# The last pass of a wide cross attention also prepares the feed-forward's first tokens and weights

## Chip, cores and metric

One core of a Trainium2 chip runs the whole program. The metric is the device time of one execution in microseconds. The engines are PE (TensorE), DVE (VectorE), ACT (ScalarE), POOL (GpSimd) and SP (SyncE, which issues the transfers). L12 is line 12 of the kernel.

## The reference

Six residual blocks run over x, 32 sequences of 64 tokens, 512 wide, each on layer-normalised tokens (`_layernorm`):

```python
x = x + _L0_attn_ref(_layernorm(x), ...)             # attention, weights by sign
x = x + _L0_xattn_ref(_layernorm(x), ctx_4096, ...)  # 32 heads of 128, 8 key heads, q and k by RMS norm
x = x + _L0_ffn_ref(_layernorm(x), c1_w, c2_w, w1, w2t)
x = x + _L1_attn_ref(...)
x = x + _L1_xattn_ref(...)
x = x + _L1_ffn_ref(...)
```

The block behind the change's boundary is the third:

```python
inter = xf @ c1_w.T @ c2_w.T                 # rank 16, 1792 wide
blk = inter.reshape(B * T, 56, 32)
idx = argmax(blk, -1) + arange(0, 1792, 32)  # one hidden unit of each 32
h = relu(einsum('bkm,bm->bk', w1[idx], xf))
out = einsum('bk,bkm->bm', h, w2t[idx])
```

## The kernel before

The 2048 tokens stay in one SBUF tensor X, 16 tiles of 128 tokens. A group is four tiles (512 tokens), `ST` = 4. Every product in full precision is made of rounded operands: a float32 matrix is kept as a rounded part ("hi", type fp32r, written by ACT) and what is left ("lo", by DVE or POOL), and three matmuls (hi·hi, hi·lo, lo·hi) make one product (`products`, L93).

The program is a row of blocks: `small_attention` ("sign"), `cross_attention`, `sparse_ffn`, `small_attention` ("alibi", "cross", and the experts). Each block writes one instruction list for each engine by hand, and the order in it is fixed. An engine waits on semaphores. Between blocks all engines wait for each other, so nothing of a block starts before the last instruction of the block before has ended on every engine.

`cross_attention` (L1945) runs 16 passes (`PASSES`): two halves of 1024 tokens (two groups each) by eight key heads. A pass loads Wq and Wo for its head through one landing buffer `raw`, each split by ACT (`wq_keep`, Wo at L2184) and POOL (`low`, L2205). Its two steps of 512 tokens make four query heads of products (`head`), their sums of squares, scores, softmax, values and then eight output products `output(0)` to `output(7)` of twelve matmuls (L2520). DVE adds each to X (`add_y`, L2327). So in pass 15 all of X's first group has been final since pass 7. A second landing buffer, `raw_kv`, takes key and value weights for two passes and the context halves; from pass 14 on it holds nothing that is still to come. `PT` takes the turned probabilities up to the end.

`sparse_ffn` (L1153) makes four passes, one for each group. A pass has 16 slots, four tiles by four quarters of 448 hidden units: PE makes the rank product (`rank_product`, L1493) one slot ahead, then H(s), the hidden product of slot s (12 matmuls on W1), then turns the kept h of slot s-2 (L1526), then the second-layer product of slot s-4 (`second`, L1471). DVE finds each block's maximum, marks it in `one_hot` (L1395), takes the first of POOL's ranks (L1403, L1405) and keeps the marked h (L1414). H(s) waits for the h kept of slot s-2 and, in the first tile, for its quarter's weights.

Ahead of the first pass stands the preparation of group 0: `ln.vector_first` (statistics, inverse and xn tile by tile, L134), ACT's four roots, four turns on PE (`x_turn`), their hi and lo parts, then `project_r(0)`, the product with C1 into H[0], which ACT and DVE split into rT, and `first_rank(0)`.

The weights come as 15 pieces through a ring of three rooms: piece n is loaded into room n % 3 once the piece before in it has been split. Pieces 0 to 7 are W1 (two for a quarter), 8 to 14 are W2. ACT rounds them in order; the tables `LOW_BY_VECTOR` and `LOW_BY_POOL` say behind which slot DVE or POOL takes the low part. The rank matrices C1 and C2 land in `h_kept` (HM); C2's two low strips of 32 rows are DVE's (L1374).

## Time and profile before

| | us |
|---|---|
| median of three runs | 2302.62 (2302.35 to 2306.49) |
| profiled execution, whole | 2299.73 |
| its span, first to last instruction | 2297.9 |
| PE busy in the span | 2207.0 (96%) |
| cross attention | about 220 to 1357 |
| feed-forward | about 1357 to 1757 |

The rows below are from the profiled execution. In a timeline row the number in brackets is how long the engine was idle before the row, and the name behind the arrow is what ended that; "PEq" there is the meeting of the engines between blocks. A row can merge several instructions of one kind (x8). A PE row's length has the fill of the array in it, so the distance of two starts is the better measure of what a matmul costs.

### The profile page before, as it was taken

What the parts mean: (1) busy time and instruction counts of PE and PEld (TensorE: products, weight loads), DVE (VectorE), ACT (ScalarE), POOL (GpSimd) and SP (SyncE); (2) the same over time, 40 slices, a digit from 0 to 9 for tenths busy, and PEclk for the clock granted to TensorE, in tenths of its full rate; (3) what the DMA queues carried; (4) which work ended last, traced back from release to release, by engine and by line L of the source; (5) the groups of instructions that cost most, each with busy time, mean ns of one, the idle gap of its engine ahead of it and who ended that gap; (6) DMA issues with size and microseconds to landing.
All of it is one profiled execution on the core that took longest, in us unless ns stands there. A gap on an engine that the chain in (4) does not pass through costs nothing. (4 is left out here: it accounts for less than half of the span.)

```text
span 2297.9 us, 39454 instructions
## 1 busy us (share of the span) xinstructions
PE 2207.0 (96%) x15918; PEld 1742.2 (76%) x15918; DVE 1376.8 (60%) x2387; ACT 1016.1 (44%) x1734; POOL 885.5 (39%) x654
## 2 busy tenths in 40 slices
PE   6997999999999999999999979999998999999998
PEld 4675877778787787877778767888887677777776
DVE  7887533344323543334433369787794888888866
ACT  6774543445435454353544442111102656666532
POOL 3575231332314324132231326121122768677621
PEclk9999999999999999999999989999999999999999
DMA  4000111110112101111010113000002000100001
GB/s 162 2 20 21 56 38 37 38 56 19 37 38 74 56 20 37 38 38 55 20 37 19 38 62 116 0 0 0 0 1 74 20 1 21 43 26 11 2 1 74
DMA packets 23032, 80.65 MB, mean 35 GB/s; under 512 B 4048, under 2 KB 6224, under 8 KB 16720
## 3 DMA queue, kind: packets, MB, share of 16 engines
q1 hardware_dynamic: 22864, 78.28, 9.8%
q8 instruction: 121, 1.98, 0.4%
q14 instruction: 47, 0.39, 0.1%
HBM read 74.08 MB, written 4.19 MB: 34 GB/s over the span
## 5 line engine op out<-in xcount | busy, mean ns | idle before, releaser
L2520 PE MATMUL xat_TP<-xat_Wo,xat_oT_hi 128*128 128x512 f32 x1024 | 322.4, 396 | 5.8 <-issue 5.8
L2218 POOL TENSOR_TENSOR xat_T<-xat_T,xat_mask 128x512 f32<-128x512 f32 x64 | 81.7, 1301 | 525.9 <-DVE xat_T L2300 525.9
L104 PE MATMUL xat_G<-xat_xnT_hi,xat_Wq 128*128 128x512 f32 x768 | 249.3, 397 | 0.0
L2520 PEld LDWEIGHTS xat_TP<-xat_Wo,xat_oT_hi 128*128 128x128 f32 x1024 | 187.3, 188 | 58.1 <-issue 22.4
L2327 DVE TENSOR_TENSOR X<-X,xat_TP 128x512 f32<-128x512 f32 x128 | 86.9, 679 | 202.5 <-PE xat_TP L2520 202.4
L2291 DVE RECIPROCAL xat_q_inv_rms<-xat_OT 128x16 f32<-128x16 f32 x32 | 8.3, 258 | 328.9 <-PE xat_OT L2447 328.9
L2520 PE MATMUL xat_TP<-xat_Wo,xat_oT_lo 128*128 128x512 f32 x512 | 199.6, 390 | 0.0
L1334 POOL TENSOR_TENSOR ffn_one_hot<-ffn_one_hot,ffn_block_rank 128x448 f32<-128x448 f32 x64 | 75.9, 1186 | 259.1 <-DVE ffn_one_hot L1395 259.1
L678 POOL TENSOR_TENSOR two_T<-two_T,two_row_max 128x512 f32<-128x512 f32 x128 | 131.6, 1051 | 113.9 <-DVE two_row_max L769 113.7
L104 PEld LDWEIGHTS xat_G<-xat_xnT_hi,xat_Wq 128*128 128x128 f32 x768 | 144.3, 188 | 34.1
L1310 ACT ACTIVATE ffn_hT_hi<-ffn_TP 128x384 fp32r<-128x384 f32 x64 | 34.9, 545 | 292.1 <-PE ffn_Y L1471 251.1
L104 PE MATMUL xat_G<-xat_xnT_lo,xat_Wq 128*128 128x512 f32 x384 | 151.8, 395 | 0.0
L1471 PE MATMUL ffn_Y<-ffn_w,ffn_hT_hi 128*128 128x512 f32 x448 | 145.6, 406 | 0.0
L687 POOL TENSOR_TENSOR two_T<-two_T,two_row_inv 128x512 f32<-128x512 f32 x128 | 133.4, 1064 | 15.2 <-DVE two_row_inv L793 14.9
L2205 POOL TENSOR_TENSOR xat_Wq<-xat_weights_raw,xat_Wq 128x2048 fp32r<-128x2048 f32 x16 | 74.0, 4624 | 153.1 <-ACT xat_Wq L2084 153.1
L104 PE MATMUL two_G<-shared_xnT_hi,shared_weights 128*128 128x512 f32 (+1 forms) x344 | 119.6, 410 | 4.7 <-PEq L1156 4.6
L564 ACT ACTIVATE two_PT<-two_TP 128x512 f32<-128x512 f32 x128 | 76.4, 597 | 92.7 <-PE two_TP L1026 92.5
L2520 PEld LDWEIGHTS xat_TP<-xat_Wo,xat_oT_lo 128*128 128x128 f32 x512 | 96.1, 188 | 20.7
L2224 POOL TENSOR_TENSOR xat_T<-xat_T,xat_row_inv 128x512 f32<-128x512 f32 x64 | 66.2, 1045 | 104.7 <-DVE xat_row_inv L2314 104.7
L2151 ACT ACTIVATE xat_qT<-xat_G 128x512 f32<-128x512 f32 x96 | 57.1, 595 | 98.0 <-PE xat_G L104 98.0
L104 PE MATMUL ffn_H<-shared_weights,shared_xnT_hi 128*128 128x448 f32 x256 | 95.4, 373 | 4.8 <-DVE ffn_h_kept L1414 4.7
L104 PE MATMUL ffn_H<-shared_weights,shared_xnT_lo 128*128 128x448 f32 x256 | 94.5, 369 | 0.0
(418 smaller groups left out, 5693.8 us busy)
## 6 DMA issues: line engine op xcount, KB each, us to landing
xat_weights_raw<-in_Cq_q SPq DMA_DIRECT2D x16, 1024.0 KB, 4.8
xat_weights_raw<-in_Cq_o SPq DMA_DIRECT2D x16, 1024.0 KB, 4.6
xat_kv_raw<-in_Cq_kv SPq DMA_DIRECT2D x7, 1024.0 KB, 7.5
two_ctxT_raw<-in_ctxT SPq DMA_DIRECT2D x8, 512.0 KB, 3.7
shared_weights_raw<-in_w1T SPq DMA_DIRECT2D x8, 448.0 KB, 4.0
shared_weights_raw<-in_w SPq DMA_DIRECT2D x7, 512.0 KB, 3.6
out<-X SPq DMA_DIRECT2D x6, 512.0 KB, 3.1
X<-in_x SPq DMA_DIRECT2D x2, 1024.0 KB, 6.9
```

Source lines behind the costliest of these rows:

```text
L104: last = eng.matmul(out, a, b, start=(n == 0), stop=(n == len(steps) - 1))
L564: eng.activation(PT[:, u % PTS, :, :, :], TP[:, :].rearrange("p (c g n) -> p c g n", c=2, g=2), ACT.Copy)\
L678: eng.tensor_tensor(row, row, mx[:, u % 4, :].unsqueeze(2).to_broadcast([P, CH, SEQ]), ALU.subtract)\
L687: eng.tensor_tensor(row, row, ri[:, s % 2, r, :].unsqueeze(2).to_broadcast([P, CH, SEQ]), ALU.mult)\
L1334: eng.tensor_tensor(e, e, rank[:, :].unsqueeze(1).to_broadcast([P, QB, BLK]), ALU.mult)\
L1471: last = eng.matmul(Y[t % 2][:, :], lhs, rhs, start=(m == 0 and lhs is h and rhs is w), stop=(m == CHUNKS - 1 and lhs is l))
L2151: eng.activation(qT[:, h, :], Q[h][:, :], ACT.Copy).then_inc(q_ready.sem, 1)
L2205: return eng.tensor_tensor(w[1][:, :, :], landed[:, :, :], w[0][:, :, :].bitcast(F32), ALU.subtract)
L2218: eng.tensor_tensor(T[:, n, :, :], T[:, n, :, :], mask[:, :].unsqueeze(1).to_broadcast([P, ROWS, SEQ]), ALU.add)\
L2224: eng.tensor_tensor(T[:, n, :, :], T[:, n, :, :], ri[:, n, :].unsqueeze(2).to_broadcast([P, ROWS, SEQ]), ALU.mult)\
L2327: eng.tensor_tensor(xt, xt, TP[m % 2][:, :], ALU.add).then_inc(y_added.sem, 1)
L2520: last = eng.matmul(TP[m % 2][:, :], x, w, start=(n == 0), stop=(n == len(steps) - 1))
```

## The change

Four tensors stay allocated where before each block had its own: `landing`, `landing2`, `rounded` and `rounded2`. Nearly all landing buffers and rounded weights of the first three blocks are views of them, placed so that what cross attention no longer reads can be overwritten with what the feed-forward needs. W1 is kept as four quarter tensors for each part. The small tensors of LayerNorm become views of one.

In cross attention's last two passes (`LAST` = 15) the engines get new steps, all for group 0 of the feed-forward:
- SP: C2 is loaded in pass 14 into what was `raw_kv`, C1 in pass 15 once C2 is split, and W1's pieces 0 and 1 (`EARLY_W1`) once Wo is split.
- ACT: C2's rounding at the end of pass 14 ahead of the next Wq, the root ahead of the q root, C1's rounding behind Wo's, and at the end hi parts and the two weight pieces.
- POOL: C1's low part behind Wo's, and the two pieces' low parts at the end.
- DVE: C2's low strips and the statistics at the head of pass 15, the four xn before `add_y(2)`, and the low parts between `add_y(4)` and `add_y(6)`.
- PE: two tiles are turned behind `output(4)`, two behind `output(5)`, into the banks of S.

The feed-forward then starts with `project_r(0)`; its SP starts with piece 2; POOL takes piece 2's low part and DVE piece 3's, and from there the two tables alternate one piece earlier.

```diff
@@ cross_attention
+        nln = LayerNorm(mem, X, ident, eps, xn=lead["xn"], kept=lead["xnT"], groups=1, small=ln.small)
+        NB = [S[0], S[1], S[0], S[1]]
...
@@ SP
                 load(raw, a["Cq_o"], g, wo_landed)
+                if j == LAST - 1:
+                    eng.wait_ge(wkv_lo.sem, wkv_lo.before(jp))
+                    eng.dma_start(c2raw, a["c2T"]).then_inc(c_landed[1].sem, 16)
+                if j == LAST:
+                    eng.wait_ge(c2_lo.sem, c2_lo.at(0, 2))
+                    eng.dma_start(c1raw, a["c1T"]).then_inc(c_landed[0].sem, 16)
+                    eng.wait_ge(wo_lo.sem, wo_lo.at(j, 1))
+                    for k in range(EARLY_W1):
+                        eng.dma_start(w1_piece(k)[0], w1_piece(k)[2]).then_inc(w1_landed[k].sem, 16)
...
@@ ACT
+                    if j == LAST and st == 0:
+                        nln.scalar_sd(eng, 0)
...
+                if j == LAST:
+                    eng.wait_ge(c_landed[0].sem, c_landed[0].at(0, 16))
+                    eng.activation(C1[0], c1raw, ACT.Copy).then_inc(c_hi.sem, 1)
                 project(1)
...
                 keep_oT(2)
+                if j == LAST - 1:
+                    eng.wait_ge(c_landed[1].sem, c_landed[1].at(0, 16))
+                    eng.wait_ge(kv_done.sem, kv_done.at(jp, KV))
+                    eng.activation(C2, c2raw, ACT.Copy).then_inc(c_hi.sem, 1)
                 if j + 1 < PASSES:
                     wq_keep(j + 1)
+                else:
+                    for k in range(EARLY_W1):
+                        nln.scalar_hi(eng, 0, k, NB[k])
+                    for k in range(EARLY_W1):
+                        eng.wait_ge(w1_landed[k].sem, w1_landed[k].at(0, 16))
+                        eng.activation(w1_piece(k)[1][0], w1_piece(k)[0], ACT.Copy).then_inc(w1_hi.sem, 1)
+                    for t in range(EARLY_W1, ST):
+                        nln.scalar_hi(eng, 0, t, NB[t])
@@ POOL
                 low(Wo, raw).then_inc(wo_lo.sem, 1)
+                if j == LAST:
+                    eng.wait_ge(c_hi.sem, c_hi.at(0, 2))
+                    eng.tensor_tensor(C1[1], c1raw, C1[0].bitcast(F32), ALU.subtract).then_inc(c1_lo.sem, 1)
...
                 if j + 1 < PASSES:
                     low_wq(j + 1)
+                else:
+                    for k in range(EARLY_W1):
+                        landed, (hi, lo), _ = w1_piece(k)
+                        eng.wait_ge(w1_hi.sem, w1_hi.at(0, k + 1))
+                        eng.tensor_tensor(lo, landed, hi.bitcast(F32), ALU.subtract).then_inc(w1_lo[k].sem, 1)
@@ DVE
+                if j == LAST:
+                    eng.wait_ge(c_hi.sem, c_hi.at(0, 1))
+                    for lo in (P // 4, 3 * P // 4):
+                        part = slice(lo, lo + P // 4)
+                        eng.tensor_tensor(C2[part, :], c2raw[part, :], C2[part, :].bitcast(F32), ALU.subtract)\
+                           .then_inc(c2_lo.sem, 1)
+                    for t in range(ST):
+                        nln.vector_stat(eng, 0, t)
+                    nln.vector_var(eng, 0)
                 invert_q(0)
...
                 invert(3)
+                if j == LAST:
+                    eng.wait_ge(c1_lo.sem, c1_lo.at(0, 1))
+                    for t in range(ST):
+                        nln.vector_xn(eng, 0, t)
                 add_y(2)
...
                 for m in range(ST, 2 * ST):
                     add_y(m)
+                    if j == LAST and m < ST + 2:
+                        for t in (2 * (m - ST), 2 * (m - ST) + 1):
+                            nln.vector_lo(eng, 0, t, NB[t])
@@ PE
                     output(m)
+                    if j == LAST and m < ST + 2:
+                        for t in (2 * (m - ST), 2 * (m - ST) + 1):
+                            if t >= 2:
+                                eng.wait_ge(nln.lo_ready.sem, nln.lo_ready.at(0, t - 1))
+                            else:
+                                eng.wait_ge(pt_ready.sem, pt_ready.at(j, U))
+                            nln.tensor_turn(eng, 0, t, NB[t])
@@ sparse_ffn
-        LOW_BY_VECTOR = {0: (4,), 1: (6,), 2: (8,)}
-        LOW_BY_POOL = {0: (5,), 1: (7,), 2: (9,), 3: (10, 11), 4: (12,), 5: (13,), 6: (14,)}
+        LOW_BY_VECTOR = {0: (3,), 1: (5,), 2: (7,), 3: (9,)}
+        LOW_BY_POOL = {0: (4,), 1: (6,), 2: (8,), 3: (10,), 4: (11, 12), 5: (13,), 6: (14,)}
...
-            low(eng, 0)
-            low(eng, 1)
+            low(eng, EARLY_W1)
...
-            ln.vector_first(eng, [I[t % 2] for t in range(ST)])
...
-            for t in range(ST):
-                x_turn(0, t)
-            eng.wait_ge(c1_lo.sem, c1_lo.at(0, 1))
             project_r(0)
-            eng.wait_ge(c2_lo.sem, c2_lo.at(0, 2))
             first_rank(0)
```

PE around the end of cross attention, before. The turns of `shared_xn` are the first tiles, `ffn_H` with `ffn_c_0` and `ffn_c_1` (C1) is `project_r(0)`, and L1493 is a rank product.

```order
L2520 MATMUL xat_TP<-xat_Wo,xat_oT_lo 128x512
L1959 UNCONDITIONAL_BRANCH
L1475 UNCONDITIONAL_BRANCH
L210 MATMUL ffn_I<-ident,shared_xn 128x128 x16
L104 MATMUL ffn_H<-shared_xnT_hi,ffn_c_0 128x512
...
L1493 MATMUL ffn_I<-ffn_c,ffn_rT 128x448
```

The same place after. `shared_landing` is xn, `shared_rounded` stands for Wo, C1, C2, W1 and the hi and lo parts alike.

```order
L211 MATMUL xat_S<-ident,shared_landing 128x128 x8
L2535 MATMUL xat_TP<-shared_rounded 128x512 x2
...
L211 MATMUL xat_S<-ident,shared_landing 128x128 x8
...
L2535 MATMUL xat_TP<-shared_rounded,xat_oT_lo 128x512
L1914 UNCONDITIONAL_BRANCH
L1434 UNCONDITIONAL_BRANCH
L104 MATMUL ffn_H<-shared_rounded 128x512 x12
L1452 MATMUL ffn_I<-shared_rounded,ffn_rT 128x448
```

The 16 turns moved from behind the boundary to between the output products.

DVE at the end of pass 15 and the head of the feed-forward, before (L2313 and L2314 are `invert`, L149 statistics, L157 xn, L228 lo parts, L1374 C2's strips, L1361 rT's split, L1222 weight low parts):

```order
L2314 RECIPROCAL xat_row_inv<-xat_row_sum 128x8
L2327 TENSOR_TENSOR X<-X,xat_TP 128x512 x2
...
L2327 TENSOR_TENSOR X<-X,xat_TP 128x512 x4
...
L228 TENSOR_TENSOR shared_xnT_lo<-ffn_I,shared_xnT_hi 128x4x128 x3
L1374 TENSOR_TENSOR ffn_c<-ffn_h_kept,ffn_c 32x1792 x2
L1361 TENSOR_TENSOR ffn_rT<-ffn_H,ffn_rT 64x512
L1222 TENSOR_TENSOR ffn_w_1<-shared_weights_raw,shared_weights 128x2x448 x2
L1393 TENSOR_REDUCE ffn_block_max<-ffn_I 128x14
```

And after (L200 is xn, L229 the lo parts, L1327 rT's split):

```order
L2313 RECIPROCAL xat_row_inv<-xat_row_sum 128x8
L189 RECIPROCAL xat_ln_small<-xat_ln_small 128x4
L200 TENSOR_SCALAR shared_landing<-X,xat_ln_small 128x512 x4
L2326 TENSOR_TENSOR X<-X,xat_TP 128x512 x2
...
L229 TENSOR_TENSOR shared_rounded<-xat_S,shared_rounded 128x4x128 x2
L2326 TENSOR_TENSOR X<-X,xat_TP 128x512
L229 TENSOR_TENSOR shared_rounded<-xat_S,shared_rounded 128x4x128 x2
L2326 TENSOR_TENSOR X<-X,xat_TP 128x512 x2
L1914 UNCONDITIONAL_BRANCH
L1323 UNCONDITIONAL_BRANCH
L1327 TENSOR_TENSOR ffn_rT<-ffn_H,ffn_rT 64x512
L1352 TENSOR_REDUCE ffn_block_max<-ffn_I 128x14
```

In the feed-forward rT's split is now DVE's first step, with no strip and no weight piece around it.

## Rows read from the trace of the kernel before

**Rows 1.** the page, part 1: busy us (share of span) x instructions

```profile
PE 2207.0 (96%) x15918; PEld 1742.2 (76%) x15918; DVE 1376.8 (60%) x2387; ACT 1016.1 (44%) x1734; POOL 885.5 (39%) x654
```

**Rows 2.** windows: length, busy us (x rows) by engine, PEclk, DMA share, GB/s

```profile
1362.00:1380.00 18.00, 10.51 (x31) 7.75 (x30) 15.63 (x15) 8.46 (x11) 6.27 (x3) 0.59 0.41 137
1380.00:1400.00 20.00, 15.65 (x76) 13.33 (x75) 19.18 (x27) 7.96 (x9) 17.72 (x9) 0.97 0.69 203
1400.00:1500.00 100.00, 99.82 (x495) 85.63 (x494) 81.17 (x129) 14.96 (x27) 30.49 (x23) 1.00 0.07 26
...
220.00:224.00 4.00, 3.78 (x10) 2.98 (x11) 3.55 (x12) 1.51 (x2) 0.00 (x0) 0.57 0.75 259
1356.00:1360.00 4.00, 0.57 (x4) 0.23 (x3) 3.20 (x8) 1.87 (x3) 0.00 (x0) 1.00 0.41 111
```

**Rows 3.** timeline of PE: start, length, line, operation, [idle before, releaser]

```profile
1338.37 1.35 PE L2479 MATMUL xat_S<-ident,xat_T 128*128 128x128 f32 x8
...
1355.95 0.39 PE L2520 MATMUL xat_TP<-xat_Wo,xat_oT_lo 128*128 128x512 f32 x1
1359.77 0.66 PE L210 MATMUL ffn_I<-ident,shared_xn 128*128 128x128 f32 x4 [3.43 <-DVE shared_xn L157]
...
1374.38 0.39 PE L104 MATMUL ffn_H<-shared_xnT_hi,ffn_c 128*128 128x512 f32 x1
1377.17 0.70 PE L1493 MATMUL ffn_I<-ffn_c,ffn_rT 128*128 128x448 f32 x2 [2.41 <-DVE ffn_rT L1361]
...
1386.26 0.47 PE L104 MATMUL ffn_H<-shared_weights,shared_xnT_hi 128*128 128x448 f32 x1 [1.60 <-DVE ffn_h_kept L1414]
...
1398.45 0.71 PE L1471 MATMUL ffn_Y<-ffn_w,ffn_hT_hi 128*128 128x512 f32 x2
```

**Rows 4.** timeline of PE, first matmuls of cross attention

```profile
220.22 0.92 PE L104 MATMUL xat_S<-xat_Wkv,xat_ctxT_hi 128*128 128x512 f32 x2 [2.67 <-PEq L259]
```

**Rows 5.** timeline of DVE, pass 15 of cross attention

```profile
1297.78 0.69 DVE L2327 TENSOR_TENSOR X<-X,xat_TP 128x512 f32<-128x512 f32 x1 [2.03 <-PE xat_TP L2520]
1312.55 0.26 DVE L2291 RECIPROCAL xat_q_inv_rms<-xat_OT 128x16 f32<-128x16 f32 x1 [14.09 <-PE xat_OT L2447]
...
1343.81 0.69 DVE L2327 TENSOR_TENSOR X<-X,xat_TP 128x512 f32<-128x512 f32 x1 [4.55 <-PE xat_TP L2520]
...
1356.38 0.69 DVE L2327 TENSOR_TENSOR X<-X,xat_TP 128x512 f32<-128x512 f32 x1 [2.03 <-PE xat_TP L2520]
```

**Rows 6.** timeline of DVE, first rows of cross attention and of the feed-forward

```profile
219.96 2.47 DVE L178 BATCH_NORM_STATS2 xat_ln_stats<-X 128x6 f32<-128x512 f32 x4 [1.68 <-PEq L259]
...
1357.38 0.69 DVE L149 BATCH_NORM_STATS2 ffn_ln_stats<-X 128x6 f32<-128x512 f32 x1 [0.32 <-PEq L1959]
...
1359.17 0.55 DVE L157 TENSOR_SCALAR shared_xn<-X,ffn_ln_mean_var,ffn_ln_rstd 128x512 f32<-128x512 f32 x1
...
1364.09 2.33 DVE L157 TENSOR_SCALAR shared_xn<-X,ffn_ln_mean_var,ffn_ln_rstd 128x512 f32<-128x512 f32 x1
...
1370.44 5.86 DVE L1374 TENSOR_TENSOR ffn_c<-ffn_h_kept,ffn_c 32x1792 fp32r<-32x1792 f32 x2 [0.90 <-ACT ffn_c L1290]
...
1383.21 2.23 DVE L1405 TENSOR_TENSOR ffn_one_hot<-ffn_one_hot,ffn_first_max 128x448 f32<-128x448 f32 x1
```

**Rows 7.** timelines of ACT (Wq, weight piece, C2) and POOL (Wq, weight piece)

```profile
1287.25 1.92 ACT L2084 ACTIVATE xat_Wq<-xat_weights_raw 128x2048 fp32r<-128x2048 f32 x1
...
1363.05 0.94 ACT L1266 ACTIVATE shared_weights<-shared_weights_raw 128x896 fp32r<-128x896 f32 x1
...
1368.72 1.69 ACT L1290 ACTIVATE ffn_c<-ffn_h_kept 128x1792 fp32r<-128x1792 f32 x1
...
1289.25 4.61 POOL L2205 TENSOR_TENSOR xat_Wq<-xat_weights_raw,xat_Wq 128x2048 fp32r<-128x2048 f32 x1 [8.84 <-ACT xat_Wq L2084]
...
1382.84 2.12 POOL L1222 TENSOR_TENSOR ffn_w<-shared_weights_raw,shared_weights 128x896 fp32r<-128x896 f32 x1 [0.37 <-ACT shared_weights L1266]
```

**Rows 8.** the page, part 6: DMA issues, KB each, median us to landing

```profile
shared_weights_raw<-in_w1T SPq DMA_DIRECT2D x8, 448.0 KB, 4.0
```

More of the change, by code:

```diff
@@ L2849, in decoder, with shared @@
[L2849 to L2868 removed]
+            def shared(name, size, dt=F32, stack=kept):
+                return stack.enter_context(nc.sbuf_tensor(f"shared_{name}", [P, size], dt))
@@ new lines, in views, with by, halves @@
+            def views(x, *sizes):
+                ends = [sum(sizes[:n + 1]) for n in range(len(sizes))]
+                return [x[:, end - size:end] for size, end in zip(sizes, ends)]
+            def by(x, k=KC):
+                return x.rearrange("p (k n) -> p k n", k=k)
+            def halves(x):
+                return x.rearrange("p (t k n) -> p t k n", t=2, k=KC)
+            W, N, A = KC * D, KC * P, KC * QW
+            landing, landing2 = shared("landing", W), shared("landing2", W + 2 * N)
```

178 lines of the change are left out of this document (76 added, 102 removed).

## The prediction

> **What bounds the kernel now.** I read the page first: PE is the engine that is busy, so only places where it waits, or runs at a lower clock, can give time back [rows 1]. The view by windows then shows where such a place is. From 1400 to 1500, inside the feed-forward, PE is busy 99.8 of 100 us. Just before, from 1362 to 1380, it is busy 10.5 of 18 us at a granted clock of 0.59 (mostly the 1.2 GHz level), and from 1380 to 1400 it is busy 15.65 of 20 [rows 2]. So the start of the feed-forward is the hole, and what is removed there ends up in the total time as long as PE has to wait for it.
>
> PE's rows at that place give the chain [rows 3]. The last output product of cross attention starts at 1355.95 and ends at 1356.34. Then PE waits 3.43 us for the first normalised tile, turns four tiles with waits between, makes the rank product (its last matmul ends at 1374.38 + 0.39 = 1374.77), waits 2.41 us until VectorE has split rT, and starts the rank and H products at 1377.17. H(0), the first hidden product, follows two rank products at about 1377.7. H(2) starts at 1386.26 and the first second-layer product at 1398.45. From there PE has no idle row. **1398.45 is the mark I compare**: whatever moves it moves the end.
>
> **What is removed.** The chain from 1356.34 to 1377.7 holds statistics, roots, normalising, turning and splitting of four tiles, then the rank product at the low clock. The first two weight pieces and both rank matrices were loaded and split beside it. VectorE's splitting of C2 alone is 5.86 us [rows 6] and stood ahead of rT's split.
>
> **What is added in cross attention, engine by engine.** PE gets 16 turns in pass 15. Eight 128x128 turns occupy 1338.37 to 1339.48 there, 1.11 us [rows 3], so 2.2 us, and I take 2.3 with the switches between kinds. This is on the path, since PE is full.
>
> Do the turns wait? VectorE's last add waits 2.03 after the 0.69 of the one before [rows 5], so an output product of 12 matmuls takes 2.72 us, 0.227 each, and output(4) ended near 1347.95 in the old trace. The first two turns come right behind it, the other two behind output(5). In that time ScalarE rounds two tiles (well under the 0.94 of a weight piece [rows 7], about 0.6 each) and VectorE adds y (0.69) and takes two low parts (about 0.7 each): some 2.8 us from output(4)'s end, while PE needs 1.1 + 2.72 = 3.8. So no wait, with 1 us in hand. ScalarE then rounds two weight pieces (0.95 each) before tiles 2 and 3; VectorE has tile 3's low part about 6.7 us after output(4), and the block's own last output ends at 10.5. POOL's two low parts (2.12 each by the nearest row [rows 7]) end at about 8 to 9. Nothing here ends after the last add.
>
> VectorE gets 5.86 (C2) and four statistics (2.47) and four aggregates, about 9 us, at the head of pass 15. There it is idle from the add at 1297.78 until 1312.55, 14.09 us by its row [rows 5]. Cover 5 us; **cost 0**. It gets four xn before add_y(2). One costs 0.55 alone and 2.33 beside a POOL operation [rows 6], so 2.3 to 9.3; one of them at most meets POOL's last normalising, so I take 4. The add at 1343.81 had 4.55 us of idle before it [rows 5], and the add ahead of it is needed only by output(4) at 1345; cost 0, at the bad end 3.
>
> ScalarE rounds C2 (1.69) ahead of pass 15's Wq (1287.25, 1.92) and POOL's Wq low part (1289.25, 4.61, ending 1293.86) follows it [rows 7]. PE wants it at 1297.6, when pass 14's last output ends. Slack 3.7, used 1.7: cost 0. Its SP loads (the Wo load waits for that low part) move 1.7 later and have 10 us. C1's low part is a quarter of the 4.61 row, 1.2 us on POOL before bias(2), where it is idle 5 us.
>
> **The new start.** The last output ends at 1356.34 + 2.3 = 1358.6, the last add at 1359.3 (0.04 + 0.69 [rows 5]). The boundary itself: VectorE started 0.32 us after the last add [rows 6], and at the earlier boundary PE started 0.26 after VectorE [rows 4, 6]; together 0.6. So the rank product runs from 1359.9, 12 x 0.227 = 2.7 us at the high clock plus 0.16 of tail, and the 2.41 us of rounding and splitting rT remain. The first rank row starts near 1365.2 and H(0) near **1365.6, 12.1 us earlier** than 1377.7.
>
> Does the rest of pass 0 follow? Now the weight stream decides. It used to run 20 us ahead of H(0); it now begins with the block at 1359.6, 6 us ahead, with only pieces 0 and 1 done. I laid the pieces out by the rows: landing 4.0 us after issue [rows 8], rounding 0.94, low part 2.12 on POOL [rows 7] or about half of that on VectorE. Three rooms, each reissued when its low part is done.
> - Pieces 2, 3, 4 land at 1363.6, 1365, 1366.5; low parts done at about 1367.2 (POOL), 1367.7 (VectorE), 1370.9 (POOL). H(1) starts at 1368 and fits.
> - Piece 5 lands at 1371 and is split on VectorE at 1373.1; h_kept(0) is ready at 1371.9. H(2) starts at 1373.2, 7.6 us after H(0); before it was 8.6.
> - H(3) waits for piece 7, 1379; H(4) starts at 1382.4 on h_kept(2).
> - H(4), three turns (about 2.8 us) and then the second-layer product near **1385.3**; pieces 8 and 9 are ready at 1380.4 and 1383.7.
>
> 1398.45 - 1385.3 = **13.1 us**. From H(0) to the mark it is 19.7 us instead of 20.8, since the clock is up and VectorE has two low parts less. Pieces 10 to 14 stay paced by the slots: piece 11's low part moves from the slot of u=3 to u=4, some 1.3 us before its use; cost 0, at most 1.5.
>
> **Against the profiled time.** 2299.73 - 13.1 = 2286.6. The median of the runs shown is 2.9 us above the profiled one, and I predict the median: 2302.62 - 13.1 = **2289.5**.
>
> **Rules weighed.** VectorE's one_hot step at 1383.21 took 2.23 us while POOL ran a low part from 1382.84 to 1384.96 [rows 6, 7]. The Trainium skill (SBUF — State Buffer, "Who interferes with whom") says that a VectorE instruction with two SBUF inputs contends with a GpSimd one that reads SBUF, and the later one blocks for the whole instruction. The trace agrees. It is behind the second rival.
>
> **Rivals.**
> 1. *The clock falls at the new boundary.* PE still idles about 1.3 us before the rank product and 2.4 after it. At the boundary into cross attention, after idle of 2.67 us, the window shows 0.57 [rows 2, 4]; here it held 1.00 up to 1360, though PE had waited since 1356.34 [rows 2]. If it falls only after the product, H(0) and H(1) take 2.4 us longer each, but H(2) has to wait for piece 5 anyway: 1.4 us lost there, nearly nothing at H(3). If it falls already for the product, 12 x 0.2 = 2.4 more: total gain about 10.8, time 2291.8. The Trainium skill (TensorE: Matmul & The Clock Gate, "What's actually happening") says that the slow state is the default and activity releases it; that speaks for this rival, since activity is only partial here.
> 2. *The weight stream or VectorE's chain is late.* The row of landings is a median; if each takes 5 us, pieces 5 and 8 in the same room come 1 and 2 us later, and if the one_hot step is blocked in each of slots 1 to 3 (2.23 instead of the 0.69 that an add of its size takes), another 1 to 2. The second-layer product starts near 1388.3: gain 10, time 2292.6.
> 3. *The moved work holds PE in pass 15* (xn before add_y(2) at its bad end, or turns 2 and 3 waiting for low parts): 3 us; gain 10, time 2292.6.
> 4. *Slower.* One mechanism: the three-room ring. A round is 4.0 + 0.95 + 2.12 = 7.1 us and room 2 needs five, so piece 14 is ready 35 us after 1359.6, near 1395; PE wants it near 1403. To end level with before it would have to come at 1416, 56 us or 11.3 a round, so a landing of over 8.2 us; at 9 us it ends 4 us slower, 2306.6. The bandwidth of this stretch speaks against it (the old stream landed in 4.0).
> 5. *The change doesn't do what it says*: the preparation is in pass 15, but the first H waits for something else as long, for instance a landing of piece 2 or 3 near the old time. The order shows nothing of the kind; time 2302, within 0.2%.
>
> **Chances.** Forecast 0.70, rival 1 0.09, rival 2 0.10, rival 3 0.05, rival 4 0.02, rival 5 0.04. What the upper cases give lies at 2291.8 to 2292.6, and the run-to-run spread of the medians (2302.35 to 2306.49) adds about a microsecond; below, if H(1) and H(2) never wait and VectorE is the only bound, 2 us more are won. Range 2286.5 to 2293.5. 0.2% is 4.6 us, about what a measurement of this kernel can tell from no change. Faster 0.93, same 0.04, slower 0.03.
>
> **What would show it.** In the new trace: 16 turns in two groups of eight between the last output products, without idle rows; the last output about 2.3 us later; H(0) about 9 us after it instead of 21; a first second-layer product near 1385; PE full after that. Wrong would be: idle rows of PE inside pass 15 (rival 3), a low granted clock from 1360 (rival 1), H(2) to H(4) released by a weight low part with waits of over 2 us each (rival 2), or the two parts after the feed-forward being longer or shorter, which I take to be untouched.

## The result: 2283.1 us, 6.3 us more gained than forecast

| | before | after |
| --- | --- | --- |
| median of the timed runs | 2302.48 (2301.14 to 2306.49, 4 runs) | 2283.11 (2282.07 to 2283.85, 4 runs) |
| profiled execution, and its span | 2299.73, 2297.9 | 2282.07, 2280.3 |

The ratio is 0.9913, 95% interval 0.9895 to 0.993. On a second chip it was 0.9912 (0.9896 to 0.9927). The sign was right. The time lies under the stated range (2286.5 to 2293.5): the gain is 19.4 us where 13.1 were forecast.

PE's timeline of the kernel after, from pass 15 of cross attention to the mark. Columns as in [rows 3]. L211 turns a tile. L104 with ffn_H is, at 1358.78, the projection's product (128x512; the prediction calls it "the rank product"), and behind it H(0) to H(4) (128x448). L1430 is the second layer.

```profile
1347.47 1.03 PE L211 MATMUL xat_S<-ident,shared_landing 128*128 128x128 f32 x8
...
1351.09 1.03 PE L211 MATMUL xat_S<-ident,shared_landing 128*128 128x128 f32 x8
...
1358.78 3.00 PE L104 MATMUL ffn_H<-shared_rounded 128*128 128x512 f32 x12 [1.19 <-PEq L1914]
1363.29 0.66 PE L1452 MATMUL ffn_I<-shared_rounded,ffn_rT 128*128 128x448 f32 x2 [1.51 <-DVE ffn_rT L1327]
1363.78 2.60 PE L104 MATMUL ffn_H<-shared_rounded 128*128 128x448 f32 x12
...
1367.54 2.67 PE L104 MATMUL ffn_H<-shared_rounded 128*128 128x448 f32 x12 [0.96 <-DVE shared_rounded L1209]
...
1373.05 4.23 PE L104 MATMUL ffn_H<-shared_rounded 128*128 128x448 f32 x12 [2.65 <-DVE shared_rounded L1209]
...
1377.66 2.59 PE L104 MATMUL ffn_H<-shared_rounded 128*128 128x448 f32 x12
...
1381.43 2.70 PE L104 MATMUL ffn_H<-shared_rounded 128*128 128x448 f32 x12 [0.54 <-DVE ffn_h_kept L1373]
...
1384.21 0.71 PE L1430 MATMUL ffn_Y<-ffn_w,shared_rounded 128*128 128x512 f32 x2
```

The two groups of eight turns stand there without an idle time. The last output ends at 1358.78 - 1.19 = 1357.59. The projection's product follows 1.19 later, and the mark stands at 1384.21, 14.24 us earlier than the 1398.45 of [rows 3]. Between the last output's end and the mark lie **26.62 us** where before had 42.11 (1356.34 to 1398.45). The waits of PE that are left are 1.19, 1.51, 0.96, 2.65 and 0.54; their releasers are the block's start, rT's low part, two low parts of W1 on VectorE, and h_kept(2).

The windows of the kernel after over the same place (length, PE's busy time, granted clock, DMA share, GB/s), to be held against the 0.59 of [rows 2]:

```profile
1358.00:1373.00 15.00, 9.16 (x40) 1.00 0.58 177
1373.00:1377.00 4.00, 3.95 (x12) 0.57 0.74 204
1377.00:1400.00 23.00, 22.29 (x113) 1.00 0.43 131
```

The clock stays at the high level through the projection's product, H(0) and H(1), and falls once, for H(2), behind the wait of 2.65 us. H(2) takes 4.23 us for the 2.6 of the others.

**Where the 19.4 us are.** The two profiled executions give four pieces, and the medians a fifth:

| piece | us | from |
| --- | --- | --- |
| from pass 15 to the mark | 13.7 | 42.11 - 26.62, less the 1.8 of the turns |
| ahead of pass 15 | 0.6 | the rest of 14.24 |
| from the mark to the next part's first product | 1.7 | 359.74 and 358.05, rows below |
| the two later parts | 1.7 | the rest of 17.6, span less span (539.7 and 538.0) |
| median less profiled execution | 1.7 | 2.75 before, 1.04 after |

Only the first was in the forecast. The third is in a stretch in which PE hardly waits in either kernel: gaps of at most 0.32 us add up to 0.8 before and 1.2 after, and the meeting of the engines at its end takes 4.59 and 4.71. Before (first the mark in [rows 3], then this row) and after:

```profile
1758.19 0.76 PE L104 MATMUL two_G<-shared_xnT_hi,shared_weights 128*128 128x512 f32 x1 [4.59 <-PEq L1156]
```

```profile
1742.26 5.92 PE L104 MATMUL two_G<-shared_rounded 128*128 128x512 f32 x19 [4.71 <-PEq L1151]
```

1758.19 - 1398.45 = 359.74, 1742.26 - 1384.21 = 358.05. The passes inside show it more evenly. The first rank products of passes 2, 3 and 4 start at 1475.27, 1568.46 and 1661.64 before, so 93.19 and 93.18 us apart, and at 1460.97, 1553.57 and 1646.17 after, 92.60 and 92.60 apart. The groups by line and shape (busy us, mean ns of one) show which instructions are shorter, those of the second layer's hi part, by 3 ns each. First before, then after:

```profile
L1471 PE MATMUL ffn_Y<-ffn_w,ffn_hT_hi 128*128 128x512 f32 x448 | 145.6, 406 | 0.0
```

```profile
L1430 PE MATMUL ffn_Y<-ffn_w,shared_rounded 128*128 128x512 f32 x448 | 144.2, 403 | 0.0
```

### The profile page after: what moved, and what is told of

Its sections match the earlier page's. It is cut to its first block and busy times, and to the rows that moved or that the text cites. A ratio compares the mean times of both kernels' runs of the same rounds, so it can differ in the third digit from the quotient of the medians.

```text
span 2280.3 us, 39454 instructions
## 1 busy us (share of the span) xinstructions
PE 2197.6 (96%) x15918; PEld 1737.2 (76%) x15918; DVE 1371.2 (60%) x2384; ACT 1014.9 (45%) x1731; POOL 885.7 (39%) x655
## 5 line engine op out<-in xcount | busy, mean ns | idle before, releaser
L2535 PE MATMUL xat_TP<-shared_rounded 128*128 128x512 f32 x1024 | 322.5, 396 | 5.8 <-issue 5.8
L104 PE MATMUL xat_G<-xat_xnT_hi,shared_rounded 128*128 128x512 f32 x768 | 249.2, 397 | 0.0
L2196 POOL TENSOR_TENSOR shared_rounded<-shared_landing,shared_rounded 128x2048 fp32r<-128x2048 f32 x39 | 179.4, 4609 | 153.1 <-ACT shared_rounded L2058 153.1
L2535 PEld LDWEIGHTS xat_TP<-shared_rounded 128*128 128x128 f32 x1024 | 187.2, 188 | 58.1 <-issue 22.4
L2535 PE MATMUL xat_TP<-shared_rounded,xat_oT_lo 128*128 128x512 f32 x512 | 199.8, 390 | 0.0
L104 PE MATMUL ffn_H<-shared_rounded 128*128 128x448 f32 (+1 forms) x816 | 181.4, 371 | 6.1 <-DVE shared_rounded L1209 3.6
L104 PEld LDWEIGHTS ffn_H<-shared_rounded 128*128 128x128 f32 x816 | 153.6, 190 | 24.9 <-issue 5.9
L104 PEld LDWEIGHTS xat_G<-xat_xnT_hi,shared_rounded 128*128 128x128 f32 x768 | 144.1, 188 | 34.4
L104 PE MATMUL xat_G<-xat_xnT_lo,shared_rounded 128*128 128x512 f32 x384 | 151.6, 395 | 0.0
L104 PE MATMUL two_G<-shared_rounded 128*128 128x512 f32 (+1 forms) x564 | 141.4, 401 | 4.9 <-PEq L1151 4.7
L1430 PE MATMUL ffn_Y<-ffn_w,shared_rounded 128*128 128x512 f32 x448 | 144.2, 403 | 0.0
L104 PEld LDWEIGHTS two_G<-shared_rounded 128*128 128x128 f32 (+1 forms) x564 | 102.8, 188 | 28.6 <-issue 6.1
```

The source lines that it names most:

```text
L104: last = eng.matmul(out, a, b, start=(n == 0), stop=(n == len(steps) - 1))
L1430: last = eng.matmul(Y[t % 2][:, :], lhs, rhs, start=(m == 0 and lhs is h and rhs is w), stop=(m == CHUNKS - 1 and lhs is l))
L2196: return eng.tensor_tensor(w[1][:, :, :], landed[:, :, :], w[0][:, :, :].bitcast(F32), ALU.subtract)
L2535: last = eng.matmul(TP[m % 2][:, :], x, w, start=(n == 0), stop=(n == len(steps) - 1))
```

## Experiments

Theory A: all of it is preparation moved off PE's path, and the forecast mis-sized that. Theory B: the preparation is worth about what was forecast, and the rest comes from something else that the change did, the new places of the tensors in memory above all. Theory C: part of it is only the difference of single executions. Each run below was timed in five rounds beside the kernel before, on one chip for each group; "before" is the median of the same rounds. "Boundary" is the time from the last output's end to the mark, "stretch" that from the mark to the first product of the next part, and "later parts" what follows up to the span's end.

### The layout alone, and single shifts of the kernel before

The new kept tensors with their views, all preparation at its old place:

```
-        nln = LayerNorm(mem, X, ident, eps, xn=lead["xn"], kept=lead["xnT"], groups=1, small=ln.small)
...
-                    for k in range(EARLY_W1):
-                        eng.dma_start(w1_piece(k)[0], w1_piece(k)[2]).then_inc(w1_landed[k].sem, 16)
...
+            eng.dma_start(c1room, a["c1T"]).then_inc(c_landed[0].sem, 16)
...
+            ln.vector_first(eng, [I[t % 2] for t in range(ST)])
```

> The change's memory alone: the kept tensors, their views and W1 in four quarters as in the kernel after, but LayerNorm, C1, C2 and all W1 pieces are prepared in the feed-forward as before. First theory (the whole gain is moved preparation): like the kernel before within 1 us, and the first second-layer product starts near 1398. Second theory (part of the gain is the new layout): the boundary is as before, but the feed-forward after it is shorter by about 2 us (so far after it runs 2.1 us shorter between the boundary and 1750), 1.4 ns on the mean second-layer product (145.6 to 144.2), ratio 0.9991. Third theory (the differences behind the boundary are only clock phases of single executions): no difference in the second-layer product's mean, medians within 1 us of before.

Measured: 2297.12 (11 runs) for 2301.76 of before, ratio 0.998 (0.9971 to 0.9989). The boundary is still long and the stretch is 357.66. The boundary, 44.8 us, is even longer than the 42.1 of before, at a lower granted clock in this execution (0.77 over 1355 to 1400, for 0.81 before): H(4) took 4.20 us for the 2.7 of the others. On another chip, asked again:

> The layout alone, a second time, on another chip. First theory (the layout gives 2 us by its second-layer products and the rest of the 4.6 was the granted clock of those executions): 2 to 3 us under before, 357.7 from the first second-layer product to the next part. Second theory (the layout gives 4.6 by a way that the rows do not show): 4 to 5 under before again.

Measured: 2299.17 for 2302.32, ratio 0.9984 (0.9975 to 0.9993), boundary 42.32, stretch 1755.11 - 1397.43 = 357.68. So the layout is worth 2.1 us in the stretch in both, and 4.6 and 3.2 by the medians. What such a difference of medians is worth, the kernel before shows against itself:

> The kernel before, unchanged, measured as if it were a changed one. The median should lie within 1 us of before's; the spread of the difference is what every other comparison of medians here has to be read against. From the first second-layer product to the first product of the next part: 359.7 as in its other execution if those rows depend on the program alone.

Measured: 2300.87 for 2302.32, ratio 0.9993 (0.9984 to 1.0002); boundary 42.21, stretch 1755.23 - 1395.55 = 359.68, beside 42.11 and 359.74 in its other execution. The rows agree within 0.1 us where the medians of one program differ by 1.45, more than the 1 that was expected. The layout's 2.1 us in the stretch are therefore real. They are not all of it: the later parts, too, are shorter with the layout alone, 2295.5 - 1757.16 = 538.3 and 2293.2 - 1755.11 = 538.1, where the two executions of before took 539.7 and 539.7. That is the 538.0 and 538.3 of the two executions of the kernel after. Of the twelve profiled executions here with the kept tensors ten took 538.0 to 538.4 (the other two 540.9 and 541.5), the five without them 539.0 to 541.7. Part of this is the granted clock at the head of the later parts, before and layout alone:

```profile
1735.00:1790.00 55.00, 46.87 (x287) 0.94 0.25 77
```

```profile
1735.00:1790.00 55.00, 46.74 (x292) 0.97 0.24 77
```

It is 0.94 in both executions of before and 0.97 in both of the layout alone. How much of the 1.4 to 1.7 us is the clock and how much the addresses is **open**. Stretch and later parts together make 3.5 to 3.8 us, which fits the medians' 4.6 and 3.2. So do the timed runs at equal clock: at a granted clock of 0.991, 0.992 and 0.993, runs of the layout alone on the first chip took 3.7, 3.4 and 1.8 us less than runs of before in the same rounds.

Is it the places alone? The kernel before with two pads, and nothing else:

```
+        mem.sb("pad0", [P, 24])
         W2 = [mem.sb(f"w2_{n}", [P, CHUNKS, D], F32R) for n in range(2)]
...
+        mem.sb("pad1", [P, 16])
         hh = mem.sb("hT_hi", [P, 2, 4 * P], F32R)
```

> The kernel before, with a pad of 96 bytes ahead of w2 and one of 64 ahead of hT_hi, so that w2, hT_hi and hT_lo stand at the same offsets modulo 128 bytes as in the kernel after (32, 32, 32 for 64, 0, 0). If the layout's effect on the second-layer products is one of alignment: their mean falls from 145.6 to about 144.2 ns and the median by 2 us, the boundary unchanged. If it is not: as before within 0.5 us.

Measured: 2298.33 for 2301.76, ratio 0.9987 (0.9979 to 0.9996), boundary 42.3. Its mark, its next part's first product and its second-layer group:

```profile
1399.05 0.71 PE L1473 MATMUL ffn_Y<-ffn_w,ffn_hT_hi 128*128 128x512 f32 x2
```

```profile
1756.77 0.77 PE L104 MATMUL two_G<-shared_xnT_hi,shared_weights 128*128 128x512 f32 x1 [4.57 <-PEq L1156]
```

```profile
L1473 PE MATMUL ffn_Y<-ffn_w,ffn_hT_hi 128*128 128x512 f32 x448 | 145.1, 405 | 0.0
```

The stretch is 357.72, and a pass takes 92.68 us: 160 bytes of padding give the whole 2.0 us with the program otherwise unchanged. The later parts took 539.0 here, with the clock at their head at 0.97, so 0.7 of the layout's 1.4 to 1.7 us. The mean of the group moved only by 1 ns of the 3 expected, so it is the starts of the products that are closer, more than each row is shorter; the group's mean is a poor measure of it, the stretch a good one. Which of the two operands? Four more shifts were meant to say. In the kernel before, w2 alone (24 floats ahead of W2, 8 behind it), then hT alone:

> The kernel before with 96 bytes ahead of w2 and 32 behind it: w2 stands at 32 modulo 128 as in the kernel after, hT_hi and hT_lo stay at 0. If the 2.0 us between the first second-layer products and the end of the feed-forward come from where the streamed operand w2 stands, they are gained here and not in the next run; if from hT, not here.

```
+        mem.sb("pad1", [P, 8])
         hh = mem.sb("hT_hi", [P, 2, 4 * P], F32R)
```

> The kernel before with 32 bytes ahead of hT_hi only: hT_hi and hT_lo stand at 32 modulo 128, w2 stays at 64. If the weight loads' operand hT sets it, the 2.0 us of the feed-forward are gained here (353.8 to 351.8 over the same products); if w2 sets it, nothing is gained.

In the kernel after, 8 floats ahead of all kept tensors, then 8 ahead of W2 alone:

> The kernel after with 32 bytes ahead of its kept tensors, so that w2, hh and hT_lo all stand at 64 modulo 128 in place of 32. If 64 under w2 is what costs the kernel before 2.0 us, they come back here; if it is the 0 under hT, nothing changes. The boundary stays as in after either way.

> The kernel after with 32 bytes ahead of w2: w2 and hT_lo stand at 64 modulo 128, hh stays at 32. So far the stretch from the first second-layer product to the next part took 357.6 to 358.1 where w2 and hT stood at the same offset (32 and 32, 64 and 64) and 358.7 to 359.7 where they did not (64 and 0, 32 and 0, 64 and 32). If unequal offsets cost it: 358.7 or more here. If not: 358.0.

| kernel | w2, hT_hi, hT_lo modulo 128 | stretch | median, before in the same rounds |
| --- | --- | --- | --- |
| before | 64, 0, 0 | 359.74 and 359.68 | |
| before, w2 shifted | 32, 0, 0 | 358.72 | 2302.59, 2301.17 |
| before, hT shifted | 64, 32, 32 | 358.99 | 2302.26, 2301.17 |
| before, both shifted | 32, 32, 32 | 357.72 | 2298.33, 2301.76 |
| after | 32, 32, 32 | 358.05 and 357.55 | 2281.1, 2302.01 |
| after, all shifted | 64, 64, 64 | 358.14 | 2283.55, 2301.17 |
| after, w2 and hT_lo shifted | 64, 32, 64 | 357.73 | 2283.46, 2302.32 |

In the kernel before each shift gives about half, 1.0 and 0.75 (their passes took 92.85 to 93.13 us). Together they would be 1.8 of the 2.0; the kernel with both pads also moves the tensors that lie between them (C1, C2, rT, the kept h) by 96 bytes, which the single shifts do not, so that they had no part in it is not shown. In the kernel after no shift takes it back, neither 64 under all three nor unequal offsets. Its two unchanged executions differ by 0.5, nearly all of it ahead of the second pass (76.76 and 76.29 us from the mark to there); the passes behind took 92.6 to 92.7 in all of its forms in the table. So neither "64 under w2" nor "unequal offsets" is the rule; that addresses are worth 2 us in this stretch is shown, by which rule is **open**. The medians of the two half shifts show no gain at all, which fits a gain of 1 us under a scatter of 1.5.

### How much is preparation, and do its halves add up?

The kernel after once more, with three others on its chip:

> The kernel after, unchanged, beside the three others on one chip. If the layout is worth 4.6 of the 19.4 us (its run alone gave 2297.1 for 2301.8), then the moved preparation is worth the other 14 to 15, and the ratio to before stays 0.991 to 0.993. If the first comparison was short of fast runs of before, it comes nearer to the forecast's 0.9943.

Measured: 2281.1 (4 runs) for 2302.01, ratio 0.9912. Boundary 1383.60 - 1357.88 = 25.72. Theory A falls: of 19 to 21 us, 13.7 to 14.6 are the boundary less the turns, and the layout alone gives 3.5 to 3.8 (2.1 in the stretch, 1.4 to 1.7 in the later parts). B stands for those, C for what is left.

Half of the move, LayerNorm ahead and all weights at the old place:

```
-            ln.vector_first(eng, [I[t % 2] for t in range(ST)])
...
+                    for t in range(ST):
+                        nln.vector_stat(eng, 0, t)
+                    nln.vector_var(eng, 0)
...
+                    for t in range(ST):
+                        nln.vector_xn(eng, 0, t)
```

> The new layout, LayerNorm of the first tokens moved into the cross attention's last pass as in the kernel after, but C1, C2 and all W1 pieces loaded and split in the feed-forward as before. If the two halves of the move add up, it gives about half of 14. If each half hides the other's wait: C2 lands near 1366, its high part is there at 1368 and VectorE's two strips at 1372 to 1374, so the first rank product starts near 1373 (1377.2 before) and the first second-layer product near 1394: 4 to 5 us less than the layout alone, median 2292.5.

Measured: 2294.42 for 2302.01, ratio 0.9972 (0.9962 to 0.9982). PE's and VectorE's rows:

```profile
1364.51 5.49 PE L104 MATMUL ffn_H<-shared_rounded 128*128 128x512 f32 x12 [6.32 <-POOL shared_rounded L1322]
1376.20 1.09 PE L1475 MATMUL ffn_I<-shared_rounded,ffn_rT 128*128 128x448 f32 x2 [6.21 <-DVE ffn_rT L1343]
```

```profile
1369.49 5.84 DVE L1356 TENSOR_TENSOR shared_rounded<-ffn_h_kept,shared_rounded 32x1792 fp32r<-32x1792 f32 x2 [10.58 <-ACT shared_rounded L1274]
1375.36 0.69 DVE L1343 TENSOR_TENSOR ffn_rT<-ffn_H,ffn_rT 64x512 fp32r<-64x512 f32 x1
```

The other half, C1, C2 and two W1 pieces ahead, and LayerNorm at the old place, tile by tile:

> The kernel after with C1, C2 and two W1 pieces prepared ahead, but LayerNorm of the first tokens in the feed-forward, tile by tile, as before. If the halves add up: the other half of 14. If each hides the other's wait: the last low part of LayerNorm comes near 1370 as before, the product of the projection follows at once, H(0) at 1375, and since the pieces are all there by then the first second-layer product near 1394.5: 4 us less than the layout alone, median 2293.

Measured: 2292.87 for 2302.01, ratio 0.9959 (0.9946 to 0.9973).

```profile
1362.61 1.12 PE L211 MATMUL ffn_I<-ident,shared_landing 128*128 128x128 f32 x4 [3.43 <-DVE shared_landing L158]
...
1369.95 4.35 PE L104 MATMUL ffn_H<-shared_rounded 128*128 128x512 f32 x12 [1.41 <-DVE shared_rounded L229]
1375.81 0.66 PE L1464 MATMUL ffn_I<-shared_rounded,ffn_rT 128*128 128x448 f32 x2 [1.51 <-DVE ffn_rT L1339]
```

The boundary is 42.1 before, 39.4 with LayerNorm ahead, 36.2 with the weights ahead and 25.7 to 26.6 with both. The halves give 2.7 and 5.9 of 15.5 to 16.4, and wherever LayerNorm is ahead the turns cost 1.8 of that in pass 15, so net 0.9 and 5.9 of 13.7 to 14.6: each alone runs into the other's chain. With LayerNorm ahead the projection waits 6.32 us for C1's low part by GpSimd, and the first rank product 6.21 for VectorE, whose C2 strips (5.84) wait for C2's landing. With the weights ahead the chain of statistics, turns and splits still stands between the last output and the product: 10.8 us for the 13.3 of before (1369.65 - 1356.34). The forecast that each would hide the other's wait held. The mark did so for the weights (1395.37 for 1394.5); for LayerNorm it came 3.6 us late (1397.56 for 1394), since C2's strips ended at 1375.33 for 1374, rT's split still stood behind them, and the first rank product started at 1376.20 for 1373.

### What paces the new boundary

No W1 piece ahead:

```
-EARLY_W1 = 2
+EARLY_W1 = 0
```

(and GpSimd splits pieces 0 and 2, VectorE piece 1).

> The kernel after, but no W1 piece is prepared ahead: EARLY_W1 = 0, pieces 0 and 1 are loaded at the feed-forward's start, the low part of piece 0 and 2 by GpSimd, of piece 1 by VectorE. LayerNorm, C1 and C2 stay ahead. First theory (the weight stream paces the first five H products): piece 1 lands near 1364, its low part is there near 1366.5, H(0) starts 2.7 later (1366.5 for 1363.8) and all behind it too; the first second-layer product at 1387 for 1384.2, median 2286. Second theory (the chain of VectorE from the rank product paces it): no more than 0.7 later, median below 2284.

Measured: 2286.29 (6 runs) for 2301.76, ratio 0.9941 (0.9929 to 0.9953).

```profile
1356.57 2.96 PE L104 MATMUL ffn_H<-shared_rounded 128*128 128x512 f32 x12 [1.20 <-PEq L1916]
...
1364.94 4.82 PE L104 MATMUL ffn_H<-shared_rounded 128*128 128x448 f32 x12 [3.09 <-DVE shared_rounded L1209]
```

From the projection's product to H(0) it takes 8.4 us for 5.0, and to the mark 28.9 for 25.4: 3.5 us, where the first theory said 2.7. H(0) itself took 4.82 us for 2.60, at a granted clock of 0.62 from 1364 to 1373: that is in the 3.5. The two early pieces are worth that. The next three kernels tried to take the waits of 0.96 and 2.65 away.

First, piece 2's low part from GpSimd to VectorE:

```
-            low(eng, EARLY_W1)
             eng.wait_ge(small.sem, small.at(0, 16))
...
                     low_r(i)
+                    low(eng, EARLY_W1)
```

> The kernel after, with the low part of piece 2 made by VectorE ahead of piece 3's in place of GpSimd. If the three-room ring paces H(1) and H(2): VectorE is idle when piece 2's high part is there (1364.2), so the room comes free at 1365.5 for 1366.5 and piece 5 lands 1 us earlier, the wait of 0.96 ahead of H(1) goes, that of 2.65 ahead of H(2) shrinks to about 1.7; the first second-layer product 1.0 us earlier, median 2282. If the chain of VectorE paces it: no gain, or 0.5 lost.

Measured: 2282.13 (6 runs) for 2301.76, ratio 0.9921. The room did come free earlier: piece 5 was rounded at 1369.12, 10.1 us behind the product's start, for 11.4 in after (1370.16). But VectorE came to its low part at 1372.02, behind the ranking chain, 13.0 us after that start for 12.9:

```profile
1369.12 0.95 ACT L1253 ACTIVATE shared_rounded<-shared_landing 128x896 fp32r<-128x896 f32 x1 [2.05 <-DMA shared_landing<-in_w1T]
```

```profile
1371.48 0.62 DVE L1373 SCALAR_TENSOR_TENSOR ffn_h_kept<-ffn_H,ffn_one_hot 128x448 f32<-128x448 f32 x1
1372.02 1.26 DVE L1209 TENSOR_TENSOR shared_rounded<-shared_landing,shared_rounded 128x896 fp32r<-128x896 f32 x1
```

H(2) waited 2.64 as before. So with the landing earlier it is VectorE's queue ahead of the low part that H(2) waits for, the second theory; in the kernel after the two end within 0.6 us of each other (the piece is rounded by 1371.11, VectorE is free at 1371.65). Next, two more pieces in the tensor of xn, loaded once the turns are done:

```
+            eng.wait_ge(nln.turned.sem, nln.turned.at(0, ST))
+            for k in range(2):
+                eng.dma_start(lead["extra"][k], a["w1T"][:, 2 * k:2 * k + 2, QW:2 * QW]).then_inc(extra_landed[k].sem, 16)
...
-        LOW_BY_VECTOR = {0: (3,), 1: (5,), 2: (7,), 3: (9,)}
+        LOW_BY_VECTOR = {0: (5,), 1: (7,)}
```

> The kernel after, with W1's pieces 2 and 3 also loaded ahead, into the tensor of xn when the four turns are done (1352), split at the head of the feed-forward by ScalarE, GpSimd (2) and VectorE (3) under the projection's product; the ring of three takes pieces 0, 1, 4, 5, ...; VectorE makes the low parts of 3, 5, 7 alone. If the ring's stream and the low parts queued on VectorE pace the first five H products: the waits of 0.96 and 2.65 ahead of H(1) and H(2) go, H(2) starts at 1370.7 for 1373.1, h_kept(2) ends at 1379.2 for 1381.4, the first second-layer product at 1382 for 1384.2, and the clock does not fall at 1373; median 2280. If GpSimd's ranking paces them: within 0.7 us of after.

Measured: 2282.84 (5 runs) for 2302.01, beside 2281.1 of after in the same rounds. The wait ahead of H(1) is gone, H(2) now waits for h_kept(0):

```profile
1370.95 2.00 POOL L1322 TENSOR_TENSOR ffn_one_hot<-ffn_one_hot,ffn_block_rank 128x448 f32<-128x448 f32 x1
```

```profile
1376.32 3.81 PE L104 MATMUL ffn_H<-shared_rounded 128*128 128x448 f32 x12 [2.16 <-DVE ffn_h_kept L1391]
```

GpSimd ranks the first block only when piece 4's low part is done. From the product to the mark it takes 24.4 us, where after took 25.4 and 24.5 in its two executions. Nothing is won that could be told apart. Then the same in another order, GpSimd's ranking first:

```
-            low(eng, 2)
-            low(eng, 4)
+            low(eng, 2)
...
-        LOW_BY_VECTOR = {0: (5,), 1: (7,)}
-        LOW_BY_POOL = {0: (6,), 1: (8,), 2: (9,),
+        LOW_BY_VECTOR = {0: (5,), 1: (7,), 3: (9,)}
+        LOW_BY_POOL = {0: (4,), 1: (6,), 2: (8,),
```

> Four early pieces as in the run before it, in another order: GpSimd ranks the first block ahead of piece 4's low part, VectorE makes rT's low part ahead of piece 3's, and VectorE takes piece 9 behind h_kept(2). If VectorE and GpSimd's ranking chain paces H(2) to H(4) (in the run before, H(2) waited 2.16 for h_kept(0), which ended 12.8 behind the start of the projection's product): h_kept(0) ends at 11.5, h_kept(2) at 21, and the first second-layer product starts 24.3 behind that start, 25.4 in after; median 1 to 2 us under after's, 2280. If the weights' stream paces them still: no gain.

Measured: 2285.43 (6 runs) for 2301.17, slower than its neighbours. h_kept(0) started 11.5 us behind the product's start, 0.8 earlier than in after. But piece 4's low part on GpSimd, behind the ranking, ended 10.9 us after that start for 7.6 in the run before, so its room was late for piece 7, and VectorE stood still:

```profile
1372.24 1.09 DVE L1217 TENSOR_TENSOR shared_rounded<-shared_landing,shared_rounded 128x896 fp32r<-128x896 f32 x1 [3.44 <-ACT shared_rounded L1267]
```

The mark is 28.1 us behind the product's start. The granted clock, too, was lower in this boundary (0.89 over 1355 to 1386, for 0.94 in the kernel after), which is in the 28.1. Stream and ranking chain both end behind PE here, by 2 to 3 us (waits of 2.65 and 2.16); taking from one gives the wait to the other. No version beat the kernel after.

## Why the prediction was right, and where it was wrong

**Right: the hole and its size.** The forecast put 26.7 us between the last output's end (1358.6) and the mark (1385.3); measured are 26.62, and 25.72 in a second execution. That it agrees within 0.1 us is in part luck: from the last output's end H(0) came 0.8 us earlier than forecast (6.2 for 7.0), from there H(2) 1.7 later (9.3 for 7.6), and from there the mark 0.9 earlier (11.2 for 12.1). Its steps:

- *16 turns on PE's path, 2.3 us.* The output behind each group starts 0.79 later (1348.26 for 1347.47) and its own pace loses another 0.1: 0.9 a group, 1.8. Neither group waited, as forecast. This is 0.5 us of the miss.
- *VectorE's 9 us at the head of pass 15 cost nothing.* They are 7.0, and 7.06 of the 14.09 us of idle in [rows 5] are left. C2's strips took 4.07 without GpSimd beside them, for the 5.86 of [rows 6]:

```profile
1297.93 4.07 DVE L2367 TENSOR_TENSOR shared_rounded<-shared_landing,shared_rounded 32x1792 fp32r<-32x1792 f32 x2
...
1311.98 0.26 DVE L2290 RECIPROCAL xat_q_inv_rms<-xat_OT 128x16 f32<-128x16 f32 x1 [7.06 <-PE xat_OT L2462]
```

- *Four xn before add_y(2), 4 us on VectorE, cost nothing.* They took 2.69, and the add behind them, with 4.55 us of idle before it in [rows 5], still had 2.55.
- *Boundary 0.6, product in 2.7 at the high clock.* 1357.59 to 1358.78 is 1.19 from PE's end to PE's start, where the forecast had 1.3 (1358.6 to 1359.9). The product took 3.0 for 2.86, at the high clock: rival 1 did not come in this form. The clock fell later, once, behind H(2)'s wait, and H(2) took 1.6 us longer for it. At the mark no cost of it shows: the form of the kernel after with 32 bytes ahead of w2 kept a granted clock of 1.00 here and took 25.2 us from the product to the mark, for 25.4 and 24.5 in the two executions of after.
- *2.41 us of gap behind the product.* It was 1.51. The two C2 strips of [rows 6] end at 1370.44 + 5.86 = 1376.30, 1.5 us behind the product's end at 1374.77, and rT's split started there. The forecast said that the strips stood ahead of the split, took their own cost away, and kept the gap that they made: 0.9 us too much. With it and the last output's end 1.0 us earlier (1357.59 for 1358.6), H(0) started at 1363.78 for 1365.6.
- *H(1) fits, H(2) at 1373.2 on piece 5, H(3) on piece 7, H(4) on h_kept(2).* H(1) waited 0.96, for a low part of 1.82 us on VectorE beside GpSimd's (1.09 in the second execution, without the wait). H(2) started at 1373.05 for 1373.2, but 2.65 us after PE was ready for it: the gap that was put too long and the stream that came too late cancelled. In VectorE's chain to it stands a one_hot step of 1.82 us beside a GpSimd low part (L1364; 0.69 in the next slot), which is rival 2's mechanism. H(3) did not wait for piece 7 at all, and H(4) waited 0.54 on h_kept(2), as forecast. What the forecast named as H(2)'s cause, piece 5's landing, is only half of it: with the landing 1 us earlier nothing changed. Then VectorE's order holds it.
- *Mark at 1385.3.* 1384.21, of which 0.6 were won ahead of pass 15 and 0.5 by cheaper turns.

**Wrong: that the work behind the mark is untouched.** Two steps failed. The prediction itself named the first as a sign of being wrong: "the two parts after the feed-forward being longer or shorter, which I take to be untouched".

The first is that I took the moved work for the whole change. Its four kept tensors move the operands of the feed-forward, and some of the parts behind it, and I gave that no term, not even as a range. The layout alone is worth 2.1 us on the stretch that I took as constant (359.7 to 357.7), shown to be the addresses by the same 2.0 us from two pads in the kernel before, and 1.4 to 1.7 us in the later parts, by addresses and clock together. In the profiled execution of the kernel after the two are 1.7 and 1.7 of the 6.3 us that were missed. I had read the views as a means and not as an edit with a price of its own.

The second is that I moved the median by the profile's difference, 2302.62 - 13.1, and let the range rest on the boundary's terms. Before's profiled execution lay 2.75 us under its median, after's 1.04, which is 1.7 us of the miss. The runs go with the granted clock: an execution has or does not have some stretches at the lower level. The windows of two executions of one and the same kernel before:

```profile
190.00:230.00 40.00, 30.45 (x238) 0.91 0.09 29
...
1340.00:1400.00 60.00, 43.57 (x186) 0.86 0.41 128
```

```profile
190.00:230.00 40.00, 30.26 (x253) 1.00 0.09 29
...
1340.00:1400.00 60.00, 43.56 (x185) 0.86 0.44 137
```

At 190 to 230, the entry into cross attention, the clock was 0.91 in one and 1.00 in the other; the spans are 2297.9 and 2294.9. At the feed-forward's start it was 0.86 in both: that one belongs to the program, and the change removed most of it (0.97). Over the 23 timed runs of before on one chip, the mean granted clock goes from 0.990 to 0.993 and the time from 2305.2 to 2299.3, some 2 us for each 0.001. These timed runs of before have a mean of 0.9917 and those of after of 0.9965. The boundary's rows (0.86 to 0.97 over 60 us, divided by the span) account for 0.0029 of these 0.0048. A little more is at the head of the later parts (0.94 and 0.97 over 55 us, so 0.0007). Why after's executions also hold the high clock more often elsewhere is **open**; the runs show that it is so, not why.

Together: 13.1 forecast, + 0.5 turns, + 0.1 at the boundary, + 0.6 ahead of pass 15, + 1.7 in the stretch (layout: addresses), + 1.7 in the later parts (layout: addresses and clock), + 1.7 between profile and median, which is 19.4. The 0.6 is no work of the change: the two executions of before differ by 3.0 there.

**The rivals.** 1 came in part (a fall behind H(2)'s wait) and made H(2) 1.6 us longer, of which the mark shows nothing. 2 came in part: low parts on VectorE did hold H(1) and H(2), for 0.96 and 2.65, and three of the first four one_hot steps were longer beside GpSimd (1.82, 1.56 and 1.38 us for 0.69); its other cause, landings of 5 us, did not come (median 4.1). 3 and 4 did not come; the ring was late by at most 2.65 us. 5 no.

## What to carry to other kernels

When a chain of preparation and a stream of weights end at the same place, moving one alone gains little (0.9 and 5.9 us here, net of the turns) and both together much more (13.7 to 14.6): cost them together, and test them apart. A change that moves buffers is two changes, and the new addresses have a price of their own, here 2 us on 1750 PE instructions; run the layout alone, and leave some us of range for it. Read a small effect in the rows of one stretch: two executions of the kernel before agreed there within 0.1 us and two of the kernel after within 0.5 (their whole passes within 0.02), where two medians of one program differed by 1.5. And read every stretch: the later parts, taken for untouched, held as much of the miss as the feed-forward.

## What was not expected of the hardware

- The places of tensors in SBUF change how closely matmuls follow each other: 359.74 us for a stretch in which PE's gaps add up to 0.8 us, and 357.72 with 160 bytes of padding ahead of the same tensors. Shifting w2 or hT alone gives a part (358.72, 358.99), and 32 bytes in two places did not bring the kernel after back to the slow form.
- The second-layer group's mean (406 and 405 ns for 359.74 and 357.72) hides most of it: the rows overlap, and it is the distance of their starts that shrinks.
- VectorE's low part of W1's piece 3 took 1.09 us in one execution of the kernel after and 1.82 in the other, by where GpSimd's row fell beside it, and C2's two strips took 4.07 us where GpSimd was idle and 5.86 beside its low part of a weight piece. The Trainium skill (SBUF — State Buffer, "Who interferes with whom") says that a VectorE instruction with two SBUF inputs contends with a GpSimd one that reads SBUF; the trace agrees.
- The clock fell at 1373 behind 2.65 us of idle in the kernel after, and not behind 1.19 and 1.51 with 3.0 us of work between. In the form with 32 bytes ahead of w2 the waits ahead of H(1) to H(3) were 0.92, 1.52 and 1.68, and the granted clock stayed at 1.00.
